# Message rows of a two-layer graph network on Trainium2: two tiles in three placed in PSUM by ScalarE, one in three added by VectorE

## What is computed

```python
# layer 0
msg  = relu(x[src] + edge_attr_64 @ W_e + b_e)
aggr = segment_sum(msg, dst, num_segments=1250)
# layer 1, with the row part of W1 applied to the nodes first (table = h @ W1h.T + b1)
m   = relu(table[src] + edge_attr_128 @ W1e.T)
agg = segment_sum(m, dst, num_segments=1250)      # W2 is applied after the sum
```

## Time and profile before

| what | value |
|---|---|
| median of 3 runs | 864.12 us |
| the profiled execution | 862.61 us |
| its span in the trace | 860.8 us |
| busy share PE, DVE, ACT, POOL | 91%, 76%, 52%, 41% |
| layer 0 edges | about 14 to 240 us |
| layer 1 edges | about 412 to 640 us |

### The profile page before, as it was taken

One profiled execution on the slowest core, in us unless ns is written; L12 is line 12 of the kernel. 1 busy time (PEld: TensorE's weight loads), 2 busy tenths in 40 slices (PEclk: granted clock), 3 DMA queues, 4 the chain that ended last, 5 costly groups with the idle time before them and its releaser, 6 DMA issues.

```text
span 860.8 us, 11403 instructions
## 1 busy us (share of the span) xinstructions
PE 787.4 (91%) x3714; PEld 623.1 (72%) x3714; DVE 656.0 (76%) x1161; ACT 449.8 (52%) x805; POOL 350.7 (41%) x381
## 2 busy tenths in 40 slices
PE   7888898899879999798879999999999999999993
PEld 5655555555469999686558877887867898989893
DVE  7999999999969924387769999999984363535365
ACT  4888888888744413211457777777761211111122
POOL 6777777777200000021877777777710000000011
PEclk9999999999989999889689999999999999999996
DMA  7999888888500050014868888888830110200011
GB/s 231 339 332 284 253 247 255 249 252 254 202 2 1 1 196 1 1 50 145 254 195 256 256 264 263 256 258 264 250 91 1 73 74 1 74 1 1 1 50 70
DMA packets 49293, 134.38 MB, mean 156 GB/s; under 512 B 8169, under 2 KB 8425, under 8 KB 48848
## 3 DMA queue, kind: packets, MB, share of 16 engines
q0 software_dynamic: 26720, 87.58, 33.9%
q1 hardware_dynamic: 22020, 45.59, 15.7%
q10 hardware_dynamic: 492, 0.45, 0.2%
HBM read 128.47 MB, written 5.12 MB: 155 GB/s over the span
## 4 chain that ended last, share of the span: by engine, by line
PE 51%; DVE 30%; issue 8%; DMA 5%; ACT 2%; POOL 2%; DVEq 0%; ACTq 0%; SPq 0%; POOLq 0%
PE banks L500 37%; DVE msg_lo L1080 10%; DVE raw L1088 7%; PE banks L527 7%; DVE hot L1074 3%; DVE attr_hl L1003 3%; PE banks L551 2%; PE banks L552 2%; DMA raw<-table_dram,src_sb 2%; DMA x_in<-in_x 2%; DMA attr_sb<-in_attr 2%; DVE agg L1103 1%; POOL raw L429 1%; DVE stats L1210 1%; DVE attr_lo L1003 1%
## 5 line engine op out<-in xcount | busy, mean ns | idle before, releaser
L429 POOL DMA_INDIRECT raw<-table_dram,src_sb x167 | 163.1, 976 | 63.7 <-issue 36.1
L429 POOL DMA_INDIRECT raw<-in_x,src_sb x167 | 159.8, 957 | 61.4 <-DVE msg_lo L1080 28.3
L451 POOL TENSOR_TENSOR moments<-moments,minus_half 128x1 f32<-128x1 f32 x32 | 20.3, 635 | 323.5 <-DVE moments L1216 323.5
L551 PE MATMUL banks<-msg_hi,hot 128*128 128x512 f32 x334 | 140.1, 419 | 11.2 <-DVE msg_lo L1080 7.5
L866 ACT ACTIVATE msg_hi<-raw 128x512 fp32r<-128x512 f32 x168 | 105.5, 628 | 66.2 <-DVE raw L1088 64.9
L552 PE MATMUL banks<-msg_lo,hot 128*128 128x512 f32 x334 | 131.6, 394 | 0.0
L1088 DVE TENSOR_TENSOR raw<-banks,raw 128x512 f32<-128x512 f32 x168 | 114.0, 679 | 11.3 <-PE banks L527 8.0
L827 ACT ACTIVATE banks<-raw 128x512 f32<-128x512 f32 x166 | 98.8, 595 | 43.6 <-DMA raw<-table_dram,src_sb 36.4
L1080 DVE SCALAR_TENSOR_TENSOR msg_lo<-raw,msg_hi 128x512 fp32r<-128x512 f32 x168 | 113.5, 676 | 3.3 <-ACT msg_hi L866 3.2
L1080 DVE SCALAR_TENSOR_TENSOR msg_lo<-banks,msg_hi 128x512 fp32r<-128x512 f32 x166 | 112.6, 678 | 2.3 <-ACT msg_hi L866 2.2
L551 PEld LDWEIGHTS banks<-msg_hi,hot 128*128 128x128 f32 x334 | 63.1, 189 | 53.4 <-DVE msg_lo L1080 41.9
(11 more groups left out here) (167 smaller groups left out, 1645.6 us busy)
## 6 DMA issues: line engine op xcount, KB each, us to landing
attr_sb<-in_attr SPq DMA_DIRECT2D x84, 128.0 KB
attr_sb<-in_attr SPq DMA_DIRECT2D x42, 256.0 KB, 4.0
Wg_raw<-in_Wg SPq DMA_DIRECT2D x3, 1536.0 KB, 6.3
W_raw<-in_W SPq DMA_DIRECT2D x2, 2048.0 KB, 14.4
raw<-in_x,src_sb POOLq DMA_INDIRECT x167, 4.5
raw<-table_dram,src_sb POOLq DMA_INDIRECT x167, 4.1
x_in<-in_x SPq DMA_DIRECT2D x5, 512.0 KB, 11.6
rows<-in_x SPq DMA_DIRECT2D x1, 2560.0 KB, 12.5
```

The costliest lines, as they stand in the source:

```text
L429: pool.indirect_dma_start(rows_of(L, t), None, tables[L], bass.IndirectOffsetOnAxis(ap=src_sb[:, t:t + 1], axis=0)).then_inc(gathered[t % ...
L551: nc.tensor.matmul(acc, h, msg_hi[L][:, t % MSG, :], start=start, stop=False)
```

## The change

Tiles whose number is divisible by 3 are added, the other two in three are placed. Of the five banks that are used for products, four are now place banks and one is the add bank. The test `odd(t)` becomes `in_bank(t)` wherever it chose the way of a tile, and the counts of placed and added tiles take the place of `t // 2`.

```diff
-RAW, ADD_BANKS, PLACE_BANKS, MSG, HOT, RING = 14, 2, 3, 6, 3, 3
+RAW, ADD_BANKS, PLACE_BANKS, MSG, HOT, RING = 14, 1, 4, 6, 3, 3
...
-        add_bank, place_bank = bank[2:4], [bank[0], bank[1], bank[6]]
+        add_bank, place_bank = [bank[2]], [bank[0], bank[1], bank[6], bank[3]]
...
+        def in_bank(t):
+
+            return t % 3 != 0
+
+        placed_tiles = [t for t in range(TILES) if in_bank(t)]
+
+        def places(t):
+
+            return len([u for u in range(t) if in_bank(u)])
+
+        def adds(t):
+
+            return t - places(t)
...
-            i = t // 2
-            return place_bank[i % PLACE_BANKS] if odd(t) else add_bank[i % ADD_BANKS]
+            return place_bank[places(t) % PLACE_BANKS] if in_bank(t) else add_bank[adds(t) % ADD_BANKS]
...
-                if t >= RAW and odd(t):
-                    pool.wait_ge(placed[L], (t - RAW) // 2 + 1)
+                if t >= RAW and in_bank(t - RAW):
+                    pool.wait_ge(placed[L], places(t - RAW) + 1)
                 elif t >= RAW:
                     pool.wait_ge(low[L], t - RAW + 1)
...
-                    nc.tensor.transpose(bank[3][:, 0:P], ident[:, :], ident[:, :])
+                    nc.tensor.transpose(bank[2][:, 0:P], ident[:, :], ident[:, :])
...
-                if odd(t):
-
-                    pe.wait_ge(placed[L], i + 1)
+                if in_bank(t):
+
+                    pe.wait_ge(placed[L], places(t) + 1)
                 else:
 
-                    wait(pe, added[L], i - ADD_BANKS + 1)
+                    wait(pe, added[L], adds(t) - ADD_BANKS + 1)
...
-                    act.wait_ge(low[L], t - 2 * PLACE_BANKS + 1)
+                    act.wait_ge(low[L], placed_tiles[i - PLACE_BANKS] + 1)
...
-                    if 2 * j + 3 < TILES:
-                        place(L, 2 * j + 3)
+                    for t in step_tiles(j + 1):
+                        if in_bank(t):
+                            place(L, t)
...
-                    if j < STEPS:
-                        add_product(L, 2 * j)
+                    for t in step_tiles(j):
+                        if not in_bank(t):
+                            add_product(L, t)
```

More of the change, by code:

```diff
@@ L506, in keep_busy @@
                 for _ in range(turns):
-                    nc.tensor.transpose(bank[3][:, 0:P], ident[:, :], ident[:, :])
+                    nc.tensor.transpose(bank[2][:, 0:P], ident[:, :], ident[:, :])
             def edge_product(L, t):
-                i, c, ks = t // 2, t // CHUNK, slice(t % CHUNK * P, (t % CHUNK + 1) * P)
+                c, ks = t // CHUNK, slice(t % CHUNK * P, (t % CHUNK + 1) * P)
                 if t % CHUNK == 0:
                     pe.wait_ge(attr_split[L], c + 1)
-                if odd(t):
-                    pe.wait_ge(placed[L], i + 1)
+                if in_bank(t):
+                    pe.wait_ge(placed[L], places(t) + 1)
                 else:
-                    wait(pe, added[L], i - ADD_BANKS + 1)
+                    wait(pe, added[L], adds(t) - ADD_BANKS + 1)
                 if L == 0:
@@ L526, in edge_product @@
                 for n, (features, W) in enumerate(passes):
-                    mm = nc.tensor.matmul(edge_bank(t), features, W, start=n == 0 and not odd(t),
-                                          stop=n == len(passes) - 1, skip_group_check=odd(t))
+                    mm = nc.tensor.matmul(edge_bank(t), features, W, start=n == 0 and not in_bank(t),
+                                          stop=n == len(passes) - 1, skip_group_check=in_bank(t))
                 mm.then_inc(add_mm[L], 1)
@@ L847, in place @@
             def place(L, t):
-                i = t // 2
+                i = places(t)
                 wait_gathered(act, L, t)
@@ L853, in place @@
                 elif i >= PLACE_BANKS:
-                    act.wait_ge(low[L], t - 2 * PLACE_BANKS + 1)
+                    act.wait_ge(low[L], placed_tiles[i - PLACE_BANKS] + 1)
                 copy(edge_bank(t), rows_of(L, t)).then_inc(placed[L], 1)
             def message_high(L, t):
-                if odd(t):
+                if in_bank(t):
                     act.wait_ge(add_mm[L], t + 1)
                 else:
-                    act.wait_ge(added[L], t // 2 + 1)
+                    act.wait_ge(added[L], adds(t) + 1)
                 wait(act, summed[L], t - MSG + 1)
-                nc.scalar.activation(msg_hi[L][:, t % MSG, :], edge_bank(t) if odd(t) else rows_of(L, t),
+                nc.scalar.activation(msg_hi[L][:, t % MSG, :], edge_bank(t) if in_bank(t) else rows_of(L, t),
                                      ACT.Relu).then_inc(relued[L], 1)
@@ L1079, in low_message @@
                 dve.wait_ge(relued[L], t + 1)
-                nc.vector.scalar_tensor_tensor(msg_lo[L][:, t % MSG, :], edge_bank(t) if odd(t) else rows_of(L, t), 0.0,
+                nc.vector.scalar_tensor_tensor(msg_lo[L][:, t % MSG, :], edge_bank(t) if in_bank(t) else rows_of(L, t), 0.0,
                                                msg_hi[L][:, t % MSG, :].bitcast(F32), ALU.max,
```

## The result

| | kernel before | kernel after |
|---|---|---|
| median | 864.55 us (863.08 to 865.61, 4 runs) | 872.45 us (870.76 to 874.87, 4 runs) |
| the profiled execution | 862.61 us, span 860.8 | 874.87 us, span 873.0 |
| last window add of layer 0 | 240.06 us | 238.89 us |
| layer 1, first gather to last rest | 408.38 to 636.30: 227.9 us | 406.33 to 648.57: 242.2 us |
| behind it to the end | 224.5 us | 224.4 us |

The ratio of after to before is 1.0085, 95% interval [1.0062, 1.0108]: the kernel is slower, where 13 us less was forecast. The profiled execution of after is the slowest of its four; its span is 12.2 us longer than that of before. Layer 0 ends 1.2 us earlier, the node update behind it takes 0.9 us less, layer 1 takes 14.3 us more. So the time was lost in the gathers' stage of layer 1, which was held to be untouched.

What follows compares the result with a forecast made beforehand. VectorE was taken to bound layer 0 (15.72 us a group) and GpSimd to set layer 1's pace (15.2 us). Gains of 12.5 us in layer 0 and 0.7 in layer 1, 13.2 together, gave 864.12 - 13.2 = 850.9 us, range 846.7 to 857.

Steps and rivals of the forecast that it cites:

- GpSimd's pace in layer 1: Layer 1's gathers: 0.962 + 0.305 us each, 15.2 us a group, unchanged by the change and not quickened by a faster VectorE.
- the 0.94 for faster: Whole kernel: summed chance of 0.94 that it gets faster by more than 0.2% (1.7 us).
- Layer 1's tail: End of layer 1, last gather to last rest, 9.9 us before: 0.7 us gained, bounds +2 to -3 us.
- VectorE's pace in layer 0: Layer 0: two adds fewer a group bring VectorE's pace from 15.72 to 14.52 us.
- cross waits: ScalarE's list: double place waits for rests six tiles back and delays a relu by 0.52 us; costed at nothing.
- Bank reads for VectorE: VectorE's rests: 682 ns from a bank, 680 from a slot, so 28 more bank reads a layer cost nothing.
- GpSimd's limit in layer 0: End of layer 0: last gather at 213.1 to 214.1 us, costing 0 to 0.7 us over VectorE's limit.
- The first steps: Start of layer 0, 38 to 56 us, where ScalarE bounds during `start_sums`: 1.3 us lost, bounds 0 to 3.
- GpSimd binding earlier: Layer 0: the 15 us from gather to rest stay, only 8 us of slot waits are won; 855.4 us, chance 0.14.
- The single add bank: Layer 1: TensorE's products wait 0.5 us each for VectorE's adds, 25 us over 14 groups; 876 us, chance 0.04.
- ScalarE as the bound: Layer 0: ScalarE needs 15.3 us a group with its waits, gain only 5 us; 858.9 us, chance 0.10.
- The slower side: Whole kernel slower, through TensorE's products waiting for VectorE's adds in layer 1; 876 us, chance 0.04.

Runs made afterwards that it cites:

- experiment 1: Changed kernel, layer 1 from tile 24: VectorE's two-SBUF instructions on 8 columns, 854.75 us; as counterpart, 10 of 26 PSUM-reading instructions on 8 columns, 868.56 us.

## Why the prediction was wrong

*GpSimd's pace in layer 1: this is the step that failed.* The prediction took 0.95 + 0.30 us a gather for granted ("start and pace are GpSimd's") and asked only whether the other engines keep up. The length of a gather depends on what VectorE does. Sized from the traces: 143 x (1.078 - 0.963) = 16.4 us over tiles 24 to 166. The evidence lay in before's own rows: the earlier trace rows has a mean of 962 ns in layer 1 and 946 in layer 0. I spread it evenly; it was one gather of some 1.14 us in every group of twelve, all 12 of them beside a rest of an added tile. The prediction's last sentence named "gathers that take longer than 0.95 us at the faster pace" as what would make it wrong, but no rival had it, and so the 0.94 for faster was far too high.

*Layer 1's tail: right in sign, too small.* The last rest comes 7.6 us after the last gather (640.96 to 648.57), before 9.9: 2.3 us won, 0.7 forecast, 3 as the bound. 16.4 - 2.3 = 14.1 us, beside the 14.3 us measured.

*VectorE's pace in layer 0: right, but not to the end.* Forecast 14.52 us a group, measured 14.60 from window add to window add for seven groups, with ScalarE busy for 13.77 us beside the 13.7 that were worked out (columns of the earlier trace rows); then three groups of 15.06, 16.61 and 17.08 us follow, in which VectorE waits 4.9 us for relus and a product, where before kept 15.72. The cover of the cross waits that was costed at nothing held in the seven: TensorE waited 18.9 us for places from 60 to 235 us, in before 7.1, and VectorE stayed full.

```profile
93.68:108.28 14.60, 13.34 (x54) 8.58 (x53) 14.41 (x23) 13.77 (x29) 10.95 (x13) 1.00 0.90 263
```

*Bank reads for VectorE: right.* The rest takes 682 ns from a bank and 687 from a slot, between 40 and 230 us. The 62 cycles of the Trainium skill (VectorE: DVE Perf Modes, The TRN2 errata) aren't there.

*GpSimd's limit in layer 0: the sum was mis-sized.* Forecast: the last gather at 213 to 214 us; measured: 223.54.

```profile
223.54 0.94 POOL L442 DMA_INDIRECT raw<-in_x,src_sb  x1 [0.30 <-issue]
...
235.93 0.68 DVE L1094 SCALAR_TENSOR_TENSOR msg_lo<-banks,msg_hi 128x512 fp32r<-128x512 f32 x1
```

From tile 24 to 166 it took 188.3 us: 142 x 1.25 = 177.5, plus 143 x 0.024 = 3.4 for meetings, plus 7.2 of slot waits, 188.1 in sum. The slot waits of before did go: they were 9.1 us, all from tile 40 on, most of them as one idle time of 0.94 us in each group (0.30 of it the usual), and the changed kernel has none behind tile 50. But it has 7.2 us of others, at five tiles from 26 to 50, with idle times up to 2.64 us, for rests of the first steps that came late. The kernel before first, at tile 90, then the changed one, at tile 50:

```profile
122.76 0.94 POOL L429 DMA_INDIRECT raw<-in_x,src_sb  x1 [0.94 <-DVE msg_lo L1080]
...
76.19 0.94 POOL L442 DMA_INDIRECT raw<-in_x,src_sb  x1 [2.64 <-DVE msg_lo L1094]
```

Tile 50 is gathered 6.2 us later than in before (69.97), and behind it 4.8 us are won back, so that the last gather comes 1.4 us later instead of 8 to 9 earlier. GpSimd has no time to spare for more. In the two traces of experiment 1 the slot waits were 2.7 and 4.2 us, and layer 0 ended 3.2 and 3.5 us earlier than in the changed kernel's own trace.

*The first steps: forecast 1.3 us lost.* The rest of tile 36 began at 75.2 us, before at 69.0, so 6.2 us. The same code had it at 70.7 and 71.4 in experiment 1, and the version that keeps the old order up to that tile had it at 74.0. Some us of the 6.2 belong to the execution and not to the change; how many belong to the change isn't settled.

*The rivals.* GpSimd binding earlier: it does end layer 0, but not for the reason given, since the distance from gather to rest fell from 15.0 to 12.4 us. The single add bank: between 440 and 640 us TensorE waited only 8.3 us, all for places, and never for VectorE's adds. ScalarE as the bound: not in steady state. The slower side was right, and the mechanism given for it was wrong.

*In sum:* with layer 0 at the 4.5 us that the other two traces show and layer 1 at 14.3 lost, less 0.9 in the node update, an estimate gives 8.9 us more, beside the 7.9 between the medians.

## What to carry to other kernels

The length of an instruction in a trace is no constant: before an engine is called the bound at a fixed pace, look at the spread behind its mean, and at what the neighbours do beside its long ones. Where two engines get in each other's way at certain moments, a change in the work of one of them can raise the number of such moments and cost more than it wins; here a gather pays for each VectorE instruction with two SBUF operands that it meets, so make the change where another engine is the bound (layer 0), keep it out where GpSimd is (layer 1), and prefer instructions that take one operand from PSUM.

## What the runs showed of the hardware

- A gather waits for a VectorE instruction with two SBUF operands that began at least 0.05 us before it and is still in flight 0.13 us after its start, and ends 0.82 us after it (1068 of 1076 cases). With an instruction that began before it, the longest wait made 0.95 into 1.47 us. Eight one-hots in layer 1 of the changed kernel that began 0.09 to 0.14 us behind the gather's start did it too:

```profile
512.28 1.63 POOL L442 DMA_INDIRECT raw<-table_dram,src_sb  x1 [0.30 <-issue]
512.41 0.67 DVE L1088 TENSOR_TENSOR hot<-iota_f,in_window 128x512 fp32r<-128x512 f32 x1
```

  0.13 + 0.67 + 0.82 = 1.62. In five other traces six rests that began there did it as well (1.55 to 1.64 us). But in layer 0 of the changed kernel 14 one-hots and 9 rests that began 0.05 to 0.14 us behind a gather's start did not; why is open.
- The other way round it costs VectorE almost nothing: one that begins together with a gather takes 0.73 instead of 0.68 us, and the gather its 0.95. Of 155 pairs with starts within 0.02 us of each other 150 left the gather at 0.95 us, and there VectorE took 0.70 to 0.74 us; in 1996 cases in which it began 0.15 to 0.75 us behind the gather's start, both took their usual 0.68 and 0.95 us. The Trainium skill (SBUF — State Buffer, SBUF: two separate sides) says that whichever starts first has the pair for its whole instruction. That agrees where VectorE is first; where the gather is first, the traces show VectorE losing some 0.05 us at most, not the rest of the gather's 0.95.

```profile
525.19 0.73 DVE L1094 SCALAR_TENSOR_TENSOR msg_lo<-raw,msg_hi 128x512 fp32r<-128x512 f32 x1 [0.83 <-ACT msg_hi L879]
525.20 0.95 POOL L442 DMA_INDIRECT raw<-table_dram,src_sb  x1 [0.30 <-issue]
```

- The same kernel takes 866 us on one chip and 961 to 969 on four others. On the late chips also TensorE's clock is lower: behind the stall shown above, in which TensorE stood for 3.5 us, the granted clock was 0.55 on average from 586 to 593 us, so for most of it at the lower of its two levels (1.2 and 2.4 GHz):

```profile
586.00:593.00 7.00, 5.60 (x16) 4.33 (x17) 5.58 (x9) 4.25 (x9) 2.63 (x3) 0.55 0.51 150
```
